# Second dispatch of a macaron layer: rounded products in place of plain ones, and the picks' weights on another engine

## The chip, the cores and the metric

The kernel runs on one core of one Trainium2 chip. The metric is the device time of one execution in microseconds (us). The five engines of the core work side by side and meet only at semaphores: TensorE (PE in the profile, with its weight loads as PEld), VectorE (DVE), ScalarE (ACT), GpSimd (POOL) and SyncE (SP, which issues transfers).

## The reference, cut to what matters

Three sublayers work on 8192 tokens of width 128: a mixture of experts, a linear attention, and the same mixture again. The change lies in the second mixture.

```python
x = x + 0.5 * ffn(layernorm(x))
x = x + attention(layernorm(x))
x = x + 0.5 * ffn(layernorm(x))

def ffn(x):                                # 8 routed experts of width 256, two picks a token
    shared = (silu(x @ shared_gate.T) * (x @ shared_up.T)) @ shared_down.T
    logits = x @ router_w.T + routing_bias
    scores, idx = top_k(sigmoid(logits), 2)
    scores = scores / scores.sum(-1)       # the weights of the picks
    w = scatter(scores at idx)
    combined = einsum((silu(x @ gate_w) * (x @ up_w)), down_w, w)
    return shared + combined
```

## The kernel before

The tokens are 16 tiles of 512 rows (TILES, TT), each of four sub-blocks of 128 (SUB). The program of each engine is written out by hand, in order; an engine does nothing ahead of its turn. There are five stages: the first dispatch (normalise, route, send each row to its two experts, shared expert), the first slot stage (72 slots of 256 rows through the routed experts), the middle, the second slot stage, and the last adds. The middle lies from about 355 to 575 us and runs the attention and the second dispatch (f = 1) together, in `TURNS`. In turn i the attention works on tile i, its projections on tile i+1, its transposes on tile i+2; the second dispatch transposes and routes tile i-1 (LAG_T) and runs the shared expert of tile i-2 (LAG_G).

Per turn, TensorE's order is: key_value(i), transpose of attention tile i+2, project(i+1, first half), ranks(i-2), gate_up(i-2, half 0), times_wo(i), transpose of dispatch tile i-1, project(i+1, second half), attend(i), router(i-1), query(i+1), gate_up(i-2, half 1), down_shared(i-3). The two halves of gate_up share one pair of banks here, so each waits for VectorE's multiply of the half before it.

VectorE's order is: mask_heads(i), add_bias(i) (the output bias), value(i+1, 0), add_late, the last steps of route for tile i-2 (from step 17 on), multiply half 0, value(i+1, 1), in some turns statistics of a late tile and three steps of the slot table, add_attention(i), norm_stats and variance for tile i, the first steps of route for tile i-1, shift_rows for tile i, in turns 4 and 8 a normaliser of four attention tiles (norm_late), multiply half 1, route up to the reciprocal (step 16), add_shared(i-3). Route is 25 small dependent steps (ROUTE_STEPS): 0 and 1 add the bias and the two column groups of the logits, 2 to 12 find the two best experts, 13 to 16 prepare the scores, 17 to 20 work out the places to which rows are sent, and 21 to 24 make the weights of the picks: product of ScalarE's Silu of the score and a reciprocal, sum of the two, reciprocal of that, and the product that is written into the rows to send.

POOL's order is, per tile: a copy of the row numbers, a wait for the whole route of that tile, four indirect transfers (first_rows) that send the rows, and then deviation: the power that makes 1/sqrt of the variance of the tile two further on, for which shift_rows waits.

ScalarE's order begins each turn with send_normalised(i-1), which needs shift_rows of the turn before, then high (the copy of the transposed attention tile), the Silu of the keys, the Silu of the scores (route_silu), the Silu of the gate, and so on.

In f = 1 the dispatch's products are plain f32 ones (the set PLAIN): `high` copies the transposed tile from tr_bank into a part of `pad`, and gate_up and router read it there as f32, the weights from `shared_raw` and `router_raw`. In f = 0 the same functions take another way: `high` copies it rounded (F32R) into xT_hi, VectorE's `low` writes the rest (the tile less xT_hi) into xT_lo, and each product is made of rounded parts: `three` is hi*hi, hi*lo and lo*hi of weights and data; the router takes two, against 16 columns that hold its weights' high and low parts. TensorE frees tr_bank for the next transpose when xT_hi is done (plain) or xT_lo is done (rounded).

Of the kernel before, what the change touches and what calls it, by code (L numbers as in the profile page):

```python
# [13 lines left out]
P = 128  # L14
# [21 lines left out]
XT_RING = 4  # L36
# [35 lines left out]
PLAIN = {(kind, 1, t) for kind in (ATTN, FFN) for t in range(TILES)}  # L72
SPLIT_BEFORE = {item: sum(other not in PLAIN for other in TRANSPOSED[:m]) for m, item in enumerate(TRANSPOSED)}
ROUTE_STEPS = 25
LOGITS_READ, MASK_STEP, SAFE_STEP, RECIP_STEP, RANKS_READ = 2, 13, 16, 17, 19
NORM_STEPS, POWER_STEPS = 10, 2
# [20 lines left out]
WARM_UP = 18  # L97
SECOND_PADDING_FROM = 22
# [16 lines left out]
def macaron(nc, x_in, w_experts, router_wT, routing_bias, w_attn, bq, bv, bo, out):  # L115
# [20 lines left out]
    with ExitStack() as ctx:  # L136
# [24 lines left out]
        shared_raw = sb("shared_raw", [P, 2 * INNER])  # L161
# [37 lines left out]
        neg_half = sb("neg_half", [P, WIDEST])  # L199
        attn_rstd = sb("attn_rstd", [P, tiles * SUB])  # L200
        attn_shift = sb("attn_shift", [P, tiles * SUB])
        xn = two("xn", [P, SUB, P])
        xT_hi = ring(XT_RING, "xT_hi", [P, TT], F32R)
        xT_lo = ring(XT_RING, "xT_lo", [P, TT], F32R)

# [101 lines left out]
        logits_psum, route_step, score_silu_done = sem("logits_psum"), sem("route_step"), sem("score_silu_done")  # L307
        ranks_psum, filled_reset = sem("ranks_psum"), sem("filled_reset")
# [51 lines left out]
        def xT_of(item):  # L360
            kind, f, t = item
            return xT_hi[t % XT_RING], xT_lo[t % XT_RING]

        def plain_xT(item):

            k = SUB * ((0 if item[0] == ATTN else 2) + item[2] % 2)
            return pad.rearrange("p e j d -> p (e j) d")[:, k:k + SUB, INPUT:RESULT]
# [117 lines left out]
        def _(sp):  # L485
# [11 lines left out]
            sp.dma_start(shared_raw[:], w_experts[0, :, 0:2 * INNER]).then_inc(attn_loaded, 16)  # L497
# [118 lines left out]
        def _(pool):  # L616
# [15 lines left out]
            pool.memset(neg_half[:], -0.5).then_inc(memsets, 1)  # L632
            pool.memset(before[:], 1.0).then_inc(memsets, 1)
            pool.memset(all_ones[:], 1.0).then_inc(memsets, 1)
            pool.wait_ge(memsets, 5)
# [7 lines left out]
            pool.wait_ge(memsets, 6)  # L643
# [23 lines left out]
            def ffn_tile(f, t):  # L667
                b = BATCH_OF[f][t]
                i = t - BATCHES[f][b][0]
                row_numbers(f, t)  # L670
                pool.wait_ge(route_step, (batch_no(f, b) + 1) * ROUTE_STEPS)
                pool.wait_ge(row_numbered, f * tiles + t + 1)
                pool.wait_ge(send_xn_done, f * tiles + t + 1)
                for j in range(SUB):
                    k = i * SUB + j
                    pool.indirect_dma_start(  # L676
                        first_rows, bass.IndirectOffsetOnAxis(ap=send_to[b % SEND_TO_RING][:, k:k + 1], axis=0),
                        send[ring_of(f, t)][:, j, :], None).then_inc(sent[ring_of(f, t)], 16)
                if f == 1 and t + LAG_G < tiles:
                    deviation(NORM_OF[(FFN, 1, t + LAG_G)][0])  # L680

# [47 lines left out]
        def _(act):  # L729
# [4 lines left out]
            def high(item):  # L734
                kind, f, t = item
                act.wait_ge(xT_psum, TR[item] + 1)
                if kind == ATTN:
                    wait_count(act, proj_psum, 3 * (t - 1))
                elif item in PLAIN:
                    act.wait_ge(gu_psum, 2 * (f * tiles + t - 2) + 2)  # L740
                elif f * tiles + t >= XT_RING:
                    act.wait_ge(gu_psum, 2 * (f * tiles + t - XT_RING) + 2)
# [36 lines left out]
            def route_silu(f, b):  # L779
                n = len(BATCHES[f][b]) * SUB  # L780
                act.wait_ge(route_step, batch_no(f, b) * ROUTE_STEPS + SAFE_STEP)
                act.activation(score_silu[:, :, 0:n], score_safe[:, :, 0:n], ACT.Silu).then_inc(score_silu_done, 1)
# [205 lines left out]
        def _(pe):  # L988
# [34 lines left out]
            def router(f, t):  # L1023
# [31 lines left out]
            def gate_up(n, c, par):  # L1055
# [32 lines left out]
            def gate_up_tile(f, t):  # L1088
                for c in range(HALVES):
                    gate_up(f * tiles + t, c, t % XT_RING)  # L1090
# [105 lines left out]
            def slot_stage(f):  # L1196
# [15 lines left out]
                if f == 0:  # L1212
                    pe.wait_ge(attn_loaded, 80)
# [75 lines left out]
            def middle():  # L1289
                first_turns()  # L1290
                for i in range(LAG_G, TURNS.stop):
# [9 lines left out]
                    if g:  # L1301
                        gate_up(tiles + i - LAG_G, 0, (i - LAG_G) % XT_RING)
# [12 lines left out]
                    if g:  # L1315
                        gate_up(tiles + i - LAG_G, 1, (i - LAG_G) % XT_RING)
# [12 lines left out]
        def _(dve):  # L1329
# [105 lines left out]
            def route(f, b, first, last):  # L1435
# [27 lines left out]
                plain = (FFN, f, ts[0]) in PLAIN  # L1463
                for step in range(first, last):
                    if plain and step == 0:
                        dve.wait_ge(logits_psum, batch_no(f, b) + 1)
                        dve.tensor_tensor(grid(z), logits[:, :, 0:ROUTED], by_expert(bias_b[:]), ALU.add
                                          ).then_inc(route_step, LOGITS_READ)
                    if plain and step < LOGITS_READ:
                        continue  # L1470
# [29 lines left out]
                    if step == 16:  # L1500
                        op = dve.reciprocal(picks(score_recip), picks(score_safe))
# [25 lines left out]
                    if step == 24:  # L1527
# [3 lines left out]
                            op0=ALU.mult, op1=ALU.mult)  # L1531
                    op.then_inc(route_step, 1)
# [250 lines left out]
            def dispatch():  # L1783
# [27 lines left out]
                for b in range(WRITTEN_OUT, len(BATCHES[f])):  # L1811
# [31 lines left out]
                    for t in ts:  # L1843
                        if t == tiles - 3:
                            dve.wait_ge(attn_loaded, 80)
# [147 lines left out]
            def first_turns():  # L1993
# [16 lines left out]
                variance(NORM_OF[(FFN, 1, 1)][0])  # L2010
                value(2, 1)
# [10 lines left out]
            def middle():  # L2022
                first_turns()
                for i in range(LAG_G, TURNS.stop):
# [7 lines left out]
                    if g:  # L2032
# [71 lines left out]
```

## Time and profile before

| | us |
|---|---|
| median of 3 runs | 793.89 (792.95 to 795.49) |
| the profiled execution, its own time | 791.14 |
| its span, first to last instruction | 789.4 |
| PE busy in the span | 694.9 (88%) |
| PEld busy | 629.6 (80%) |
| DVE busy | 551.2 (70%) |
| ACT busy | 462.1 (59%) |
| POOL busy | 453.7 (57%) |

Busy shares over the whole span mix five stages. The page's second part cuts the span into 40 slices of 19.7 us: slices 18 to 28 are the middle. There PE stands at 8 or 9 tenths and more, DVE at 8, ACT at 5 to 7 and POOL at 2 to 5. A start in the timelines is in us from the start of the span. A plain f32 product shows as two matmul records for each one written, a rounded one as one.

### The profile page before, as it was taken

Reading aid. Unit: us, or ns where it says so; the run is one execution under the profiler, and the core shown is the slowest. Engines: PE = TensorE matmul, PEld = TensorE weight load, DVE = VectorE, ACT = ScalarE, POOL = GpSimd, SP = SyncE. Lnnn points to the kernel's source line nnn. Section 1 sums busy time; section 2 is a strip of 40 time slices with the busy share of each in tenths; the row PEclk is TensorE's granted clock in tenths of the full one; section 3 lists DMA queues with packets and bytes.
Section 4 is the critical chain, followed back from the end, with each engine's and each line's share of the span. In section 5 each row is a group of like instructions: output and inputs, shape, how many; then the busy total and the mean of one; then the engine's idle time right before and its main releaser. Section 6 shows DMA issues by size and latency. Waiting matters only on the chain. (4 is left out here: it accounts for less than half of the span.)

```text
span 789.4 us, 18023 instructions
## 1 busy us (share of the span) xinstructions
PE 694.9 (88%) x5165; PEld 629.6 (80%) x5165; DVE 551.2 (70%) x1762; ACT 462.1 (59%) x849; POOL 453.7 (57%) x499
## 2 busy tenths in 40 slices
PE   4578859979999899999898999999789999899990
PEld 4466748869999899987676777777589999889990
DVE  6778887874555555688888888888865555555672
ACT  2325535237667657786775757755447677657760
POOL 5253666637777757765234353453527777667772
PEclk8579988989999999999999999999989999999995
DMA  9211164126788577651110000000427788476677
GB/s 277 84 44 42 55 165 118 43 83 190 206 246 220 167 190 196 176 168 48 51 50 30 22 28 18 26 28 19 110 71 220 215 233 241 143 195 170 186 238 232
DMA packets 88099, 103.52 MB, mean 131 GB/s; under 512 B 12228, under 2 KB 70468, under 8 KB 88004
## 3 DMA queue, kind: packets, MB, share of 16 engines
q1 hardware_dynamic: 72388, 65.23, 31.3%
q0 software_dynamic: 15616, 37.14, 13.1%
q8 instruction: 46, 0.75, 0.4%
q14 instruction: 49, 0.40, 0.2%
HBM read 51.83 MB, written 50.49 MB: 130 GB/s over the span
## 5 line engine op out<-in xcount | busy, mean ns | idle before, releaser
L676 POOL DMA_INDIRECT first_rows<-send,send_to x128 | 125.7, 982 | 170.6 <-DVE send L1528 135.9
L1862 DVE TENSOR_TENSOR h<-silu_g,u_bank 128x512 f32<-128x512 f32 x144 | 99.0, 688 | 142.8 <-ACT silu_g L870 138.4
L688 POOL DMA_INDIRECT second_rows<-row_ring x144 | 139.0, 965 | 67.5 <-issue 42.4
L688 POOL DMA_INDIRECT y_rows<-row_ring x144 | 141.2, 981 | 58.0 <-issue 35.7
L845 ACT ACTIVATE slot_gu<-w_gu 128x1024 fp32r x132 | 139.8, 1059 | 41.9 <-issue 41.8
L1190 PE MATMUL y_bank<-w_dn,h 128*128 x1152 | 151.7, 274 | 0.3 <-DVE h L1862 0.3
L1190 PEld LDWEIGHTS y_bank<-w_dn,h 128*128 128x128 f32 x1152 | 140.4, 191 | 0.5 <-issue 0.5
L991 PE MATMUL g_bank<-xT_hi,slot_gu 128*128 128x256 f32 x264 | 85.9, 325 | 12.7 <-DVE xT_lo L1853 12.7
L870 ACT ACTIVATE silu_g<-g_bank 128x512 f32<-128x512 f32 x144 | 83.6, 581 | 15.5 <-PE g_bank L993 15.4
L1084 PEld LDWEIGHTS y_bank<-w_dn,h 128*128 128x128 f32 x512 | 65.2, 202 | 23.2 <-issue 22.5
L1084 PE MATMUL y_bank<-w_dn,h 128*128 128x128 f32 x512 | 66.5, 286 | 13.2 <-DVE x L1427 13.2
L766 ACT ACTIVATE silu_g<-g_bank 128x512 f32<-128x512 f32 x64 | 38.2, 596 | 67.9 <-PE u_bank L993 43.2
L991 PE MATMUL u_bank<-xT_hi,slot_gu 128*128 128x256 f32 x264 | 75.1, 284 | 0.0
L992 PE MATMUL u_bank<-xT_lo,slot_gu 128*128 128x256 f32 x264 | 75.1, 284 | 0.0
L992 PE MATMUL g_bank<-xT_lo,slot_gu 128*128 128x256 f32 x264 | 74.7, 283 | 0.0
L993 PE MATMUL g_bank<-xT_hi,slot_gu 128*128 128x256 f32 x264 | 74.6, 282 | 0.0
L993 PE MATMUL u_bank<-xT_hi,slot_gu 128*128 128x256 f32 x264 | 74.3, 282 | 0.0
L775 ACT ACTIVATE send<-x,shift,rstd 128x128 f32<-128x128 f32 x128 | 52.1, 481 | 30.2 <-DVE shift L1405 22.6
L991 PEld LDWEIGHTS g_bank<-xT_hi,slot_gu 128*128 128x128 f32 x264 | 50.3, 191 | 14.6 <-DVE xT_lo L1853 14.6
L992 PEld LDWEIGHTS g_bank<-xT_lo,slot_gu 128*128 128x128 f32 x264 | 50.8, 192 | 0.0
L993 PEld LDWEIGHTS u_bank<-xT_hi,slot_gu 128*128 128x128 f32 x264 | 50.6, 192 | 0.0
L993 PEld LDWEIGHTS g_bank<-xT_hi,slot_gu 128*128 128x128 f32 x264 | 50.3, 190 | 0.0
(258 smaller groups left out, 1531.0 us busy)
## 6 DMA issues: line engine op xcount, KB each, us to landing
row_ring<-second_rows SPq DMA_DIRECT2D x66, 258.0 KB
row_ring<-first_rows SPq DMA_DIRECT2D x66, 132.0 KB
w_raw<-w_experts SPq DMA_DIRECT2D x21, 256.0 KB, 2.8
second_rows<-pad SPq DMA_DIRECT2D x16, 258.0 KB
x<-x_in SPq DMA_DIRECT2D x16, 256.0 KB, 7.0
xT_hi<-y_rows SPq DMA_DIRECT2D x16, 256.0 KB, 2.9
xT_lo<-y_rows SPq DMA_DIRECT2D x16, 256.0 KB, 2.9
out<-x SPq DMA_DIRECT2D x16, 256.0 KB
```

Source lines behind the costliest of these rows:

```text
L676: pool.indirect_dma_start(first_rows, bass.IndirectOffsetOnAxis(ap=send_to[b % SEND_TO_RING][:, k:k + 1], axis=0), send[ring_of(f, t)][:, ...
L688: pool.indirect_dma_start(to, bass.IndirectOffsetOnAxis(ap=rows[k][:, j, at:at + 1].bitcast(I32), axis=0), rows[k][:, j, columns], None).t ...
L766: act.activation(silu_g[c][:], g_bank[gate_bank(n, c)][:], ACT.Silu).then_inc(silu_done, 1)
L775: last = act.activation(send[ring_of(f, t)][:, j, INPUT:RESULT], x_sub(t, j), ACT.Identity, bias=bias, scale=scale)
L845: act.activation(slot_gu[n % 2][:].rearrange("p a n -> p (a n)"), w_gu[:, bass.ds(e, 1)].rearrange("p e a n -> p (e a n)").bitcast(F32), A ...
L870: act.activation(silu_g[n % 2][:], g_bank[n % 2][:], ACT.Silu).then_inc(slot_silu_done, 1)
L991: pe.matmul(bank_ap, w_parts[0], x_parts[0], start=True, stop=False)
L992: pe.matmul(bank_ap, w_parts[0], x_parts[1], start=False, stop=False)
L993: return pe.matmul(bank_ap, w_parts[1], x_parts[0], start=False, stop=True)
L1084: last = pe.matmul(shared_bank[:, s], h[t % 2][c][:, s], w_dn[:, 0, c, :], start=(c == 0), stop=(c == HALVES - 1))
L1190: last = pe.matmul(y_bank[par][:, j * P:(j + 1) * P], h[par][0][:, c * ROWS + j * P:c * ROWS + (j + 1) * P], w_dn[:, bass.ds(e[j % len(e)] ...
L1862: dve.tensor_tensor(h[par][0][:], silu_g[par][:], u_bank[par][:], ALU.mult).then_inc(slot_h_done, 1)
```

## The change

In the second dispatch the products of the shared expert and of the router become rounded ones, as in the first: PLAIN keeps only the attention's tiles. For that xT_hi and xT_lo are used as a ring of two, VectorE gets `low` for each tile (after multiply half 0, and once in first_turns), and route gets its step 0 and 1 apart instead of one add. Route on VectorE ends for f = 1 at step 20 and steps 21 to 24 go to POOL: `pick_weights`, five instructions, each of which waits for the one before it, placed in ffn_tile after the copy of the row numbers and before the wait for route. The reciprocal of the sum is there a power with the exponent -1, and the factor 0.5 is a multiplication of the sum by 2. ScalarE's route_silu and VectorE's step 16 wait for the weights of the tile before. The load of shared_raw falls away, with its wait. One constant (minus_one) is set at the start.

```diff
-XT_RING = 4
+XT_RING = (4, 2)
-PLAIN = {(kind, 1, t) for kind in (ATTN, FFN) for t in range(TILES)}
+PLAIN = {(ATTN, 1, t) for t in range(TILES)}
+PLACES_STEP = 20
+WEIGHT_STEPS = 5
...
-            sp.dma_start(shared_raw[:], w_experts[0, :, 0:2 * INNER]).then_inc(attn_loaded, 16)
...
+            pool.memset(minus_one[:], -1.0).then_inc(memsets, 1)
...
             def ffn_tile(f, t):
                 b = BATCH_OF[f][t]
                 i = t - BATCHES[f][b][0]
                 row_numbers(f, t)
+                if f == 1:
+                    pick_weights(t)
+                    pool.wait_ge(weights_step, WEIGHT_STEPS * (t + 1))
                 pool.wait_ge(route_step, (batch_no(f, b) + 1) * ROUTE_STEPS)
...
+            def pick_weights(t):
+                n = SUB
+                picks = [a[:, :, 0:n] for a in (score_silu, score_recip, prob)]
+                pool.wait_ge(score_silu_done, batch_no(1, t) + 1)
+                pool.wait_ge(route_step, batch_no(1, t) * ROUTE_STEPS + RECIP_STEP + 1)
+                pool.tensor_tensor(picks[2], picks[0], picks[1], ALU.mult).then_inc(weights_step, 1)
+                pool.wait_ge(weights_step, WEIGHT_STEPS * t + 1)
+                pool.tensor_tensor(total[:, 0:n], prob[:, 0, 0:n], prob[:, 1, 0:n], ALU.add).then_inc(weights_step, 1)
+                pool.wait_ge(weights_step, WEIGHT_STEPS * t + 2)
+                pool.tensor_scalar(total[:, 0:n], total[:, 0:n], 2.0, None, ALU.mult).then_inc(weights_step, 1)
+                pool.wait_ge(weights_step, WEIGHT_STEPS * t + 3)
+                pool.tensor_tensor(inv_total[:, 0:n], total[:, 0:n], minus_one[:], ALU.pow).then_inc(weights_step, 1)
+                pool.wait_ge(weights_step, WEIGHT_STEPS * t + 4)
+                wait_count(pool, sent[ring_of(1, t)], sent_count(1, t - SEND_RING))
+                pool.tensor_tensor(send[ring_of(1, t)][:, :, WEIGHT:WEIGHT + PICKS].rearrange("p s w -> p w s"), picks[2],
+                                   inv_total[:, 0:n].unsqueeze(1).to_broadcast([P, PICKS, n]), ALU.mult).then_inc(weights_step, 1)
...
             def route_silu(f, b):
                 n = len(BATCHES[f][b]) * SUB
                 act.wait_ge(route_step, batch_no(f, b) * ROUTE_STEPS + SAFE_STEP)
+                if f == 1:
+                    wait_count(act, weights_step, WEIGHT_STEPS * b)
...
-                    if (FFN, f, t) in PLAIN:
-                        last = pe.matmul(logits[:, 0:ROUTED], plain_xT((FFN, f, t))[:, j, :], router_raw[:], start=True, stop=True)
-                        continue
-                    pe.matmul(logits, xT_hi[t % XT_RING][:, s], router_parts[:], start=True, stop=False)
-                    last = pe.matmul(logits, xT_lo[t % XT_RING][:, s], router_parts[:], start=False, stop=True)
+                    hi, lo = xT_of((FFN, f, t))
+                    pe.matmul(logits, hi[:, s], router_parts[:], start=True, stop=False)
+                    last = pe.matmul(logits, lo[:, s], router_parts[:], start=False, stop=True)
...
-                if (FFN, 1, n - tiles) in PLAIN:
-                    xs = plain_xT((FFN, 1, n - tiles))
-                    pe.matmul(by_sub(g_bank[k][:]), shared_raw[:, c * P:(c + 1) * P], xs, start=True, stop=True)
-                    pe.matmul(by_sub(u_bank[k][:]), shared_raw[:, INNER + c * P:INNER + (c + 1) * P], xs, start=True, stop=True
-                              ).then_inc(gu_psum, 1)
-                    return
                 w = w_gu[:, 0]
-                xs = (xT_hi[par][:], xT_lo[par][:])
+                hi, lo = xT_of((FFN, n // tiles, n % tiles))
+                xs = (hi[:], lo[:])
...
                     if step == 16:
+                        if f == 1:
+                            wait_count(dve, weights_step, WEIGHT_STEPS * ts[0])
                         op = dve.reciprocal(picks(score_recip), picks(score_safe))
...
+                    if f == 1 and step == PLACES_STEP:
+                        op.then_inc(route_step, ROUTE_STEPS - PLACES_STEP)
+                        break
                     op.then_inc(route_step, 1)
...
                 variance(NORM_OF[(FFN, 1, 1)][0])
+                low((FFN, 1, 0))
                 value(2, 1)
...
                         if i - LAG_G == tiles - 1:
                             table_piece(1, "last tile")
+                    if tr:
+                        low((FFN, 1, i - LAG_T))
                     if 0 < i + 1 < tiles:
                         value(i + 1, 1)
```

## Rows read from the trace of the kernel before

**Rows 1.** Windows, one a turn: us, each engine's busy time, PE clock, DMA share, GB/s

```profile
402.84:414.87 12.03, 12.03 (x77) 9.34 (x77) 10.74 (x41) 8.61 (x19) 4.73 (x6) 1.00 0.20 64
414.87:429.98 15.11, 12.56 (x78) 9.36 (x77) 12.81 (x53) 8.37 (x19) 5.15 (x6) 1.00 0.07 23
...
516.89:528.92 12.03, 12.03 (x77) 9.34 (x77) 10.23 (x42) 7.25 (x15) 5.16 (x7) 1.00 0.07 24
```

**Rows 2.** Timeline of PE in one turn: start us, us, engine line op

```profile
455.17 1.02 PE L1063 MATMUL g_bank<-pad,shared_raw 128*128 128x512 f32 x2
...
456.88 1.95 PE L1084 MATMUL y_bank<-w_dn,h 128*128 128x128 f32 x16
...
461.01 1.10 PE L1063 MATMUL g_bank<-pad,shared_raw 128*128 128x512 f32 x2
...
462.81 0.61 PE L1254 MATMUL y_bank<-attn_raw,kv_sb 128*128 128x128 f32 x4
...
465.44 0.96 PE L1034 MATMUL route_bank<-router_raw,pad 128*128 128x8 f32 x8
466.26 1.10 PE L1237 MATMUL u_bank<-pad,attn_raw 128*128 128x512 f32 x2
```

**Rows 3.** Timeline of PE in the first dispatch, and the window over it

```profile
100.17 0.48 PE L991 MATMUL g_bank<-xT_hi,w_gu 128*128 128x512 f32 x1
...
103.06 1.95 PE L1084 MATMUL y_bank<-w_dn,h 128*128 128x128 f32 x16
...
105.19 0.26 PE L1036 MATMUL route_bank<-router_parts,xT_hi 128*128 128x16 f32 x1
...
106.09 0.66 PE L1013 MATMUL tr_bank<-ident,send 128*128 128x128 f32 x4
...
100.00:110.00 10.00, 9.54 (x65) 8.09 (x63) 9.13 (x27) 4.59 (x10) 7.70 (x9) 1.00 0.22 60
```

**Rows 4.** Timeline of DVE in the same turn as rows 2

```profile
453.54 0.68 DVE L1422 TENSOR_TENSOR h<-silu_g,u_bank 128x512 f32<-128x512 f32 x1
454.15 0.42 DVE L1914 TENSOR_TENSOR v_sb<-u_bank,bv_b 128x256 f32<-128x256 f32 x1
...
456.73 0.19 DVE L1467 TENSOR_TENSOR z<-route_bank,bias_b 128x32 f32<-128x32 f32 x1
456.96 0.19 DVE L1481 TENSOR_REDUCE score<-z 128x4 f32<-128x32 f32 x1
...
464.53 0.18 DVE L1519 TENSOR_REDUCE send_to<-pick_place 128x4 int32<-128x32 f32 x1
...
465.44 0.68 DVE L1422 TENSOR_TENSOR h<-silu_g,u_bank 128x512 f32<-128x512 f32 x1
```

**Rows 5.** Timeline of the loop through DVE, ACT and POOL, one turn

```profile
497.58 0.16 DVE L1405 SCALAR_TENSOR_TENSOR shift<-stats,rstd 128x4 f32<-128x4 f32 x1
...
500.07 0.20 ACT L782 ACTIVATE score_silu<-score_safe 128x8 f32<-128x8 f32 x1
...
502.91 1.06 POOL L676 DMA_INDIRECT first_rows<-send,send_to  x1 [5.22 <-DVE send L1528]
504.27 0.95 POOL L676 DMA_INDIRECT first_rows<-send,send_to  x1 [0.30 <-issue]
...
507.76 1.06 POOL L658 TENSOR_TENSOR rstd<-var,neg_half 128x4 f32<-128x4 f32 x1
```

**Rows 6.** POOL's small instructions: timeline, then lines' ns min/median/max

```profile
2.35 0.29 POOL L627 TENSOR_SCALAR_AFFINE_SELECT ident<-ident 128x128 f32<-128x128 f32 x1 [0.16 <-POOL ident L625]
...
L664 POOL COPY send<-number x32: 179/184/277, 13.8 to 564.5; 128x4 int32<-128x4 int32 x32
...
L658 POOL TENSOR_TENSOR rstd<-var,neg_half x17: 1046/1057/2959, 81.6 to 554.5; 128x4 f32<-128x4 f32 x15, 128x16 f32<-128x16 f32 x2
...
L694 POOL TENSOR_TENSOR w_gu<-w_raw,w_gu x8: 1266/1286/1308, 49.3 to 128.0; 128x512 fp32r<-128x512 f32 x8
```

**Rows 7.** Timeline of DVE at the end of the middle

```profile
560.78 0.19 DVE L1467 TENSOR_TENSOR z<-route_bank,bias_b 128x32 f32<-128x32 f32 x1 [0.60 <-PE route_bank L1034]
```

More of the change, by code:

```diff
@@ L97 @@
 WARM_UP = 18
+WEIGHT_STEPS = 5
+ATTN_LOADS = 4
 SECOND_PADDING_FROM = 22
@@ L160, in macaron @@
         slot_gu = two("slot_gu", [P, 2, 2 * INNER], F32R)
-        shared_raw = sb("shared_raw", [P, 2 * INNER])
         attn_raw = sb("attn_raw", [P, 4 * P])
@@ L199, in macaron @@
         neg_half = sb("neg_half", [P, WIDEST])
+        minus_one = sb("minus_one", [P, SUB])
         attn_rstd = sb("attn_rstd", [P, tiles * SUB])
@@ L202, in macaron @@
         xn = two("xn", [P, SUB, P])
-        xT_hi = ring(XT_RING, "xT_hi", [P, TT], F32R)
-        xT_lo = ring(XT_RING, "xT_lo", [P, TT], F32R)
+        xT_hi = ring(XT_RING[0], "xT_hi", [P, TT], F32R)
+        xT_lo = ring(XT_RING[0], "xT_lo", [P, TT], F32R)
         send_ring = sb("send", [P, SEND_RING, SUB, RESULT])
@@ L307, in macaron @@
         logits_psum, route_step, score_silu_done = sem("logits_psum"), sem("route_step"), sem("score_silu_done")
+        weights_step = sem("weights_step")
         ranks_psum, filled_reset = sem("ranks_psum"), sem("filled_reset")
@@ L361, in xT_of @@
             kind, f, t = item
-            return xT_hi[t % XT_RING], xT_lo[t % XT_RING]
+            return xT_hi[t % XT_RING[f]], xT_lo[t % XT_RING[f]]
         def plain_xT(item):
-            k = SUB * ((0 if item[0] == ATTN else 2) + item[2] % 2)
+            k = SUB * (item[2] % 2)
             return pad.rearrange("p e j d -> p (e j) d")[:, k:k + SUB, INPUT:RESULT]
@@ L632, in _ @@
             pool.memset(neg_half[:], -0.5).then_inc(memsets, 1)
+            pool.memset(minus_one[:], -1.0).then_inc(memsets, 1)
             pool.memset(before[:], 1.0).then_inc(memsets, 1)
             pool.memset(all_ones[:], 1.0).then_inc(memsets, 1)
-            pool.wait_ge(memsets, 5)
+            pool.wait_ge(memsets, 6)
             pool.affine_select(out=before[:], in_=before[:], compare_op=ALU.is_ge, fill=0.0, base=-1,
@@ L642, in _ @@
                                pattern=[[-HEAD, HEADS], [0, HEAD]], channel_multiplier=1).then_inc(memsets, 1)
-            pool.wait_ge(memsets, 6)
+            pool.wait_ge(memsets, 7)
             pool.affine_select(out=heads, in_=heads, compare_op=ALU.is_ge, fill=0.0, base=HEAD - 1,
@@ L738, in high @@
                     wait_count(act, proj_psum, 3 * (t - 1))
[L739 to L742, printed above, removed]
+                elif f * tiles + t >= XT_RING[f]:
+                    act.wait_ge(gu_psum, 2 * (f * tiles + t - XT_RING[f]) + 2)
                 if item in PLAIN:
@@ L1053, in ranks, with gate_up @@
                 last.then_inc(ranks_psum, 1)
-            def gate_up(n, c, par):
+            def gate_up(n, c):
                 k = gate_bank(n, c)
@@ L1089, in gate_up_tile @@
                 for c in range(HALVES):
-                    gate_up(f * tiles + t, c, t % XT_RING)
+                    gate_up(f * tiles + t, c)
             def dispatch():
@@ L1212, in slot_stage @@
                 if f == 0:
-                    pe.wait_ge(attn_loaded, 80)
+                    pe.wait_ge(attn_loaded, 64)
                     project(0, 0)
@@ L1301, in middle @@
                     if g:
-                        gate_up(tiles + i - LAG_G, 0, (i - LAG_G) % XT_RING)
+                        gate_up(tiles + i - LAG_G, 0)
                     if attn:
@@ L1315, in middle @@
                     if g:
-                        gate_up(tiles + i - LAG_G, 1, (i - LAG_G) % XT_RING)
+                        gate_up(tiles + i - LAG_G, 1)
                     if 0 <= i - LAG_G - 1 < tiles - 1:
@@ L1461, in chosen @@
                     return mask[len(ts)][:, 0:n, w * ROUTED:(w + 1) * ROUTED]
-                plain = (FFN, f, ts[0]) in PLAIN
                 for step in range(first, last):
[L1465 to L1470, printed above, removed]
                     if step > 0:
@@ L1844, in dispatch @@
                         if t == tiles - 3:
-                            dve.wait_ge(attn_loaded, 80)
+                            dve.wait_ge(attn_loaded, 64)
                             dve.tensor_scalar(bq_scaled[:], bq_col[:], SCALE, None, ALU.mult).then_inc(bq_ready, 1)
```

## The prediction

> **What bounds the kernel now.** I read the page's 40 slices first, to find the stage that the edit touches, and then only that stage: the windows cut at the start of each query product, so that one window is one turn; after that the timelines of PE, DVE and POOL inside one turn. The change touches the middle alone (the second dispatch runs there, between 355 and 575 us), so whatever bounds the slot stages stays as it is.
>
> [...] The reader is to see that two turns 114 us apart have the same 12.03 to the hundredth: a stage that waits for data wanders, one that is bound by an engine doesn't. DVE is busy for 10.2 to 10.7 us of it, and between its 41 or 42 instructions lie gaps of some 0.04 where one depends on the other [rows 1, 4], so DVE is close behind. Turn 4 is another kind: 15.11 us, PE busy for 12.56 and idle for the rest, because VectorE's normaliser of four tiles stands ahead of a multiply that PE needs; turn 8 is the same. Nine turns are ordinary ones (the first and the eighth of them stand in rows 1), two are long; three come ahead of them and two behind, where the pipeline fills and drains.
>
> A third thing is nearly as long as the turn: a loop through three engines. Shift_rows at 497.58 lets ScalarE normalise the next tile; behind that in ScalarE's order stands the Silu of the scores, which ends at 500.27; then come VectorE's places and weights, POOL's first transfer at 502.91, three more, and the power at 507.76, which ends at 508.82 and lets the next shift_rows go [rows 5]. That is 11.27 us with a hop of 0.03. It is not what ends last now, but it has under 0.8 us to spare.
>
> **The change part by part.**
>
> Gate and up on PE. Now the two halves of a tile take 456.88 - 455.17 = 1.71 and 462.81 - 461.01 = 1.80, together 3.51 us [rows 2]. Rounded, the same two halves took 103.06 - 100.17 = 2.89 us in the first dispatch, with the clock at 1.00 there too [rows 3]. So a turn of PE loses 0.62 us.
>
> Router on PE. Now 466.26 - 465.44 = 0.82 [rows 2]; rounded, 106.09 - 105.19 = 0.90 [rows 3]. It gains 0.08. PE's turn becomes 12.03 - 0.62 + 0.08 = 11.49 us, 0.54 less. Over nine turns that is 4.9 us, if nothing else is longer than 11.49.
>
> VectorE. It gains `low`, a 128x512 instruction out of PSUM; the multiply of that size holds the engine for 454.15 - 453.54 = 0.61. It gains one more step of route, 456.96 - 456.73 = 0.23. It loses steps 21 to 24: the multiply behind them starts at 465.44, the last step that stays starts at 464.53 and takes 0.18, and an instruction that doesn't depend on it may follow before its end, so between 0.73 and 0.91 goes, and I take 0.8 [rows 4]. The net is +0.04 a turn, between -0.07 and +0.11. I take nothing for it in the ordinary turns, where PE covers it, and 0.1 in all for the two long ones. If that cover is gone, eleven turns cost 0.4 us.
>
> The wait that is new on PE. Router needs `low`, and `low` stands behind multiply half 0. Now router and multiply start together, both at 465.44 [rows 2, 4]. After the change router can't start before multiply and low are through: 0.61, 0.68 for low as for the multiply, and a hop of 0.05, so 1.34 us after the multiply's start. Behind it on PE's queue wait query, gate_up half 1 and down_shared; for gate_up half 1 waits multiply half 1, which VectorE reaches only behind 13 steps of route, so VectorE isn't held up. PE pays this once, when the order first settles (turns 1 to 3, where DVE is behind), and keeps the distance from then on: PE's own way from gate_up half 0 to router (1.80 - 0.31, then times_wo, transpose, project and attend, 462.81 to 465.44 in rows 2) is 4.1 us, and behind the half's 1.49 Silu, multiply, high and low, each of some 0.6 to 0.7, two of them side by side on two engines, fit into it. Cost +1.3 us, once; between 0 (VectorE is early, so that low is done first) and 2.5 (it is paid again behind each long turn). I take 1.3.
>
> The weights on POOL. Five instructions that wait for one another and for the Silu of the scores, ahead of the four transfers and the power. The trace shows no such form of POOL with eight columns. The nearest rows: a copy of four columns 0.18 (median), a power of four columns 1.06, a dependent gap of 0.16, a two-input subtraction of 512 columns 1.29, which is 2.5 ns a column, so that eight columns are next to nothing and the fixed part counts [rows 6]. Below: four at 0.18 and a power, no gaps: 1.8 us. Above: four at 0.29 (the 128-column select) with a gap of 0.16 each, the power and its gap: 3.0 us. I take four at 0.21, gaps of 0.1 to 0.16, the power 1.06: 2.4 us. The loop is then 500.27 - 497.58 = 2.69, the weights 2.4, the issue gap of 0.30 that lies before a transfer, and from the first one's start to the next shift (the power's end and the hop) 508.85 - 502.91 = 5.94: 11.33 us [rows 5]. It stays under PE's 11.49 by a hair; the cover is gone from 2.56 us of weights on. VectorE's own route doesn't wait for the weights any more, and places (step 20) are done before them.
>
> [...]
>
> The end of the middle. Tile 15's routing is the chain: VectorE waits for the router's logits before 560.78 [rows 7], and all that follows, up to the slot table, is VectorE's. On it come low and its hop, 0.75, and one step, 0.23; off it go half a gate_up ahead of the transpose, 0.31, and steps 21 to 24, 0.8: -0.1 us.
>
> The rest. The transfer of shared_raw lies among the first loads, away from the chain: nothing. ScalarE's high writes the same 512 columns: nothing. The memset lies before POOL's first wait: nothing.
>
> The sum: -4.9 + 1.3 + 0.1 - 0.1 = -3.6 us. The profiled execution took 791.14 us, its span 789.4 and 1.7 around it; it would become 787.5. It is itself 2.75 under the median of the three runs, 793.89. Against that median, which is what the change will be compared with, I forecast 790.3 us.
>
> **The rivals.**
>
> POOL's loop becomes the bound, mildly. With weights of 2.6 to 3.1 us the loop is 11.5 to 12.0, and nine turns gain between 4.9 and 0.3; with the 1.3 the total runs from -3.6 to +1.0, say 793 us. For it: the loop is already 11.27 and the new instructions all depend on one another [rows 5]. Against: with a price in the middle of the bounds the loop stays under PE's turn, and VectorE's places and weights no longer stand between the Silu and the first transfer in one queue.
>
> POOL's loop becomes the bound, hard: slower. If the weights take 3.5 us, the loop is 12.43, longer than the turn of before: nine turns at +0.4, and 1.3 and -0.1: +4.8, 798.7 us. It decides from weights of about 3.2 us on. [...] Against it: every short instruction of POOL in the trace lies under 0.3 us and the power varies by 1% at four columns [rows 6].
>
> The router's wait costs nothing and VectorE follows PE at once: -6 us and somewhat more, 787.5 us. For it: VectorE sheds its weights just before the multiply, so the multiply comes earlier by 0.8. Against: in rows 2 and 4 the two start together, so low is late by more than that.
>
> The change doesn't shorten PE: the rounded products keep to 2.89 us in the first dispatch where PE isn't pressed; in the middle their weight loads (three per product instead of two) could stand in the way, and a turn stays near 12.0. Then only the costs are left, +1, 795 us. Against: there PE ran them back to back with the loads beside them [rows 3].
>
> **How the numbers follow.** Forecast 0.52 at 790.3 us, its own spread 788.5 to 792.5 by the bounds of VectorE's net and of the router's wait. Mild loop 0.22 at 793; hard loop 0.10 at 798.7; more gained 0.11 at 787.5; no shorter PE 0.05 at 795. A measurement of this kernel tells about 0.3%, 2.4 us, from no change, so faster means under 791.5: four fifths of the forecast's chance, all of the larger gain and a little of the mild loop: 0.55. Slower, over 796.3: the hard loop and a little beside: 0.11. Between: 0.34. The range from 786.5 to 796.5 leaves out most of the hard loop and the far end of the larger gain, together under 2 in 10.
>
> **What would show it.** Right: windows cut at query are 11.4 to 11.6 us in the nine turns, PE busy throughout; gate_up's two halves 2.9 us together; router starting right behind xT_lo, some 1.3 us after multiply half 0; POOL's five instructions 2.2 to 2.6 us from the Silu's end to the last. Wrong: DVE idle before shift_rows for POOL's power in every turn, and turns of 11.8 us or more (the loop); PE idle before router in every turn, with DVE busy throughout (VectorE's order is the bound); long turns that grow by more than 0.2.

## The result, and the profile after

The changed kernel takes 810.75 us (median of 4 runs, 808.08 to 811.89), beside 793.42 (791.95 to 795.49, 4 runs) for the kernel before: a ratio of 1.021, interval 1.0165 to 1.0256. The forecast was 790.3, up to 796.5. The profiled execution has a span of 809.1 us, 19.7 more than before.

Nearly all of it lies in the middle. The windows cut at the query products, as in [rows 1] (columns: us, busy time of PE, PEld, DVE, ACT and POOL with their instructions, PE clock, DMA share, GB/s); the last line is the tail, from the last query to the second slot stage's first `low`:

```profile
437.90:450.91 13.01, 12.04 (x82) 10.15 (x81) 10.72 (x40) 8.56 (x19) 7.06 (x11) 1.00 0.06 21
504.99:517.39 12.40, 12.03 (x82) 10.15 (x81) 10.33 (x41) 8.56 (x19) 7.07 (x11) 1.00 0.07 23
517.39:529.79 12.40, 12.04 (x82) 10.15 (x81) 10.04 (x40) 8.56 (x19) 7.06 (x11) 1.00 0.07 23
554.60:594.94 40.34, 29.60 (x173) 25.12 (x172) 29.71 (x121) 13.60 (x27) 24.25 (x36) 0.87 0.27 71
```

Turns of 12.40 us in a row, and of 13.0 where a late tile is added; before, both kinds took 12.03 to 12.21. The same to the hundredth from turn to turn, and yet PE isn't busy throughout: something else than PE sets it. The waits over the whole middle name it (columns: us in total, times, longest):

```profile
POOL prob L694 <- DVE place L1518: 71.6, 16, 8.8
...
DVE shift L1422 <- POOL rstd L662: 21.3, 14, 2.2
```

The second of them in the kernel before:

```profile
DVE shift L1405 <- POOL rstd L658: 4.3, 7, 1.0
```

So before, VectorE's shift_rows waited 4.3 us in all for POOL's power; now it waits 21.3. The loop of [rows 5], in one turn after:

```profile
511.01 0.16 DVE L1422 SCALAR_TENSOR_TENSOR shift<-stats,rstd 128x4 f32<-128x4 f32 x1 [1.28 <-POOL rstd L662]
...
513.50 0.20 ACT L806 ACTIVATE score_silu<-score_safe 128x8 f32<-128x8 f32 x1
...
514.23 0.22 DVE L1518 TENSOR_TENSOR place<-route_bank,filled 128x64 f32<-128x64 f32 x1
...
514.60 0.20 POOL L694 TENSOR_TENSOR prob<-score_silu,score_recip 128x8 f32<-128x8 f32 x1 [3.46 <-DVE place L1518]
514.88 0.20 POOL L696 TENSOR_TENSOR total<-prob 128x4 f32<-128x4 f32 x1
515.17 0.23 POOL L698 TENSOR_SCALAR total<-total 128x4 f32<-128x4 f32 x1
515.48 1.04 POOL L700 TENSOR_TENSOR inv_total<-total,minus_one 128x4 f32<-128x4 f32 x1
516.59 0.21 POOL L703 TENSOR_TENSOR send<-prob,inv_total 128x8 f32<-128x8 f32 x1
517.40 1.11 POOL L683 DMA_INDIRECT first_rows<-send,send_to  x1 [0.60 <-POOL send L703]
...
522.31 1.06 POOL L662 TENSOR_TENSOR rstd<-var,neg_half 128x4 f32<-128x4 f32 x1
...
523.40 0.16 DVE L1422 SCALAR_TENSOR_TENSOR shift<-stats,rstd 128x4 f32<-128x4 f32 x1 [1.60 <-POOL rstd L662]
```

From shift to the Silu's end 513.70 - 511.01 = 2.69, as before. Then 0.90 in which nothing of the loop runs on POOL; the weights, 516.80 - 514.60 = 2.20; a gap of 0.60; and 523.40 - 517.40 = 6.00 to the next shift. Together 12.39: this is the turn. The 0.90 is the surprise, and the row names its cause: the first weight waits for VectorE's place add. `pick_weights` waits for `RECIP_STEP + 1` = 18 steps of route, so for steps 0 to 17. The reciprocal, which it needs, is step 16; it is done at a count of 17, and 17 is what the constant `RECIP_STEP` holds. Step 17 is the place add, and this stands on VectorE behind add_shared, mask_heads, add_bias, value and, in the turns with a late tile, an add_late.

### The profile page after: what moved, and what is told of

It reads as the page before. It is cut to its first block, busy times and chain, and to the rows that moved or that the text cites. A ratio compares the mean times of both kernels' runs of the same rounds, so it can differ in the third digit from the quotient of the medians.

```text
span 809.1 us, 18241 instructions
## 1 busy us (share of the span) xinstructions
PE 704.3 (87%) x5229; PEld 652.7 (81%) x5229; DVE 553.4 (68%) x1730; ACT 461.8 (57%) x849; POOL 485.5 (60%) x580
## 4 chain that ended last, share of the span: by engine, by line
PE 42%; POOL 18%; DVE 13%; issue 9%; DMA 3%; ACT 3%; SPq 1%; POOLq 0%; DVEq 0%; ACTq 0%
PE y_bank L1207 11%; POOL first_rows L683 6%; POOL second_rows L712 6%; PE g_bank L1015 4%; PE g_bank L1017 3%; PE g_bank L1016 3%; PE u_bank L1015 3%; PE u_bank L1016 3%; PE u_bank L1017 3%; PE y_bank L1101 3%; DMA row_ring<-second_rows 2%; POOL rstd L662 2%; POOL inv_total L700 2%; DVE h L1439 2%; PE route_bank L1161 1%
## 5 line engine op out<-in xcount | busy, mean ns | idle before, releaser
L1016 PEld LDWEIGHTS u_bank<-xT_lo,slot_gu 128*128 128x128 f32 x264 | 50.5, 191 | 0.0
```

Of the source, the lines that this page charges most:

```text
L1016: pe.matmul(bank_ap, w_parts[0], x_parts[1], start=False, stop=False)
```

## The experiments

All compared with the kernel before on the same chip. For each profiled execution I cut the middle by the starts of the query products on PE: the first four turns; the nine ordinary turns of the prediction; the two long ones; and the tail. Medians and ratios come from the timed runs; the stretches (us) from one profile each. The kernel before had a median of 793.42, 792.1, 794.15 and 792.34 us in the four sessions: beside the changed kernel, e1 to e4, e5 to e8, and e9 and e10.

| kernel | first four | nine ordinary | two long | tail | middle | median | ratio (interval) |
|---|---|---|---|---|---|---|---|
| before | 38.13 | 108.04 | 29.64 | 34.08 | 209.89 | 793.42 | |
| changed | 41.53 | 114.63 | 31.92 | 40.34 | 228.42 | 810.75 | 1.021 (1.0165 to 1.0256) |
| e1_wait16 | 40.63 | 107.99 | 29.89 | 37.83 | 216.34 | 797.67 | 1.006 (1.0033 to 1.0087) |
| e2_products | 43.61 | 108.18 | 30.81 | 36.48 | 219.08 | 800.45 | 1.0102 (1.0063 to 1.0141) |
| e3_weights | 40.50 | 111.06 | 34.21 | 38.76 | 224.53 | 809.4 | 1.0202 (1.0157 to 1.0246) |
| e4_weights16 | 37.44 | 108.60 | 30.16 | 34.28 | 210.48 | 794.67 | 1.0028 (1.0004 to 1.0052) |
| e5_after_early | 41.90 | 102.63 | 29.44 | 34.38 | 208.35 | 788.89 | 0.9944 (0.9918 to 0.9969) |
| e6_before_early | 38.14 | 107.85 | 27.85 | 33.20 | 207.04 | 790.09 | 0.9954 (0.9928 to 0.9979) |
| e7_wait16_early | 41.88 | 102.62 | 29.36 | 34.27 | 208.13 | 789.82 | 0.9941 (0.9919 to 0.9962) |
| e8_plain_router | 38.08 | 102.00 | 29.29 | 34.31 | 203.68 | 786.22 | 0.9917 (0.9885 to 0.9948) |
| e10_router_alone | 39.74 | 106.87 | 29.74 | 38.89 | 215.24 | 795.4 | 1.0033 (1.0004 to 1.0063) |

### The wait, and each half of the change

**e1_wait16**, the changed kernel with one number less:

```diff
-                pool.wait_ge(route_step, batch_no(1, t) * ROUTE_STEPS + RECIP_STEP + 1)
+                pool.wait_ge(route_step, batch_no(1, t) * ROUTE_STEPS + RECIP_STEP)
```

> The changed kernel, but POOL's first weight instruction waits for step 16 of route (the reciprocal) and not for step 17 (the places), which VectorE makes only behind value and the late add. Theory A (the loop through shift_rows, ScalarE, VectorE's places, POOL's weights, transfers and power sets the turn, 12.40 us, and 13.0 where a late tile is added): the first weight instruction starts 0.8 us earlier in ordinary turns and 1.4 in those with a late add, turns of 11.5 to 11.7 us, 794 to 798 us in all. Theory B (low ahead of router, with VectorE as the bound, is what costs): turns stay at 12.4 and more, 808 to 812 us.

12 us of the middle come back (228.42 to 216.34). POOL now waits for ScalarE's Silu, and starts 0.08 behind its end (518.47):

```profile
518.27 0.20 ACT L806 ACTIVATE score_silu<-score_safe 128x8 f32<-128x8 f32 x1
...
518.55 0.26 POOL L694 TENSOR_TENSOR prob<-score_silu,score_recip 128x8 f32<-128x8 f32 x1 [2.66 <-ACT score_silu L806]
...
521.48 1.17 POOL L683 DMA_INDIRECT first_rows<-send,send_to  x1 [0.61 <-POOL send L703]
```

The ordinary turns are 11.69 to 11.84, those with a late add 12.0: theory A holds. But 797.67 is still 7 above the forecast, so the wait isn't all.

**e2_products** leaves the weights on VectorE: the call of `pick_weights` and all waits for it go, and route runs to step 24 again.

```diff
-                if f == 1:
-                    pick_weights(t)
-                    pool.wait_ge(weights_step, WEIGHT_STEPS * (t + 1))
...
-                    if f == 1 and step == PLACES_STEP:
-                        op.then_inc(route_step, ROUTE_STEPS - PLACES_STEP)
-                        break
```

> Rounded products and low as in the change, but the weights stay on VectorE (steps 21 to 24), POOL as before. Theory A: POOL's loop is that of before, VectorE has 0.8 us more a turn than in the change, turns of 11.4 to 12.3 us, 792 to 797 us in all. Theory B (low ahead of router costs): 803 us or more, TensorE idle ahead of router in each turn.

It lands between the two, so neither theory had the total: the rounded products alone cost 9.2 us in the middle, 5.5 of it in the first four turns. In the sum the nine ordinary turns gain nothing, but they aren't alike: the first takes 14.03, the next three 12.11 to 12.13, the last five 11.38 to 11.82. The loop isn't what costs here, since shift_rows waits only 0.3 us in all for the power. What theory B named does: TensorE waits ahead of the router for `low`, 13 times and 14.9 us in all over the middle. One of the first waits, and the sum from 400 to 560 us:

```profile
393.67 0.38 PE L1053 MATMUL route_bank<-router_parts,xT_hi 128*128 128x16 f32 x1 [3.40 <-DVE xT_lo L1428]
...
PE route_bank L1053 <- DVE xT_lo L1428: 8.6, 10, 1.8
```

**e3_weights** does the other half: products plain as before, weights on POOL with the change's wait. **e4_weights16** is the same with the wait for step 16. Both are the kernel before with only the weights' part of the change. Seen from the changed kernel, the products' part is taken back, of which this line is the core:

```diff
-PLAIN = {(ATTN, 1, t) for t in range(TILES)}
+PLAIN = {(kind, 1, t) for kind in (ATTN, FFN) for t in range(TILES)}
```

> Plain products as before, the weights on POOL with the change's own waits. Theory A: the loop is as long as in the change, 12.4 us in ordinary turns and 13.0 with a late add, though VectorE has 0.8 us less work a turn: 801 to 807 us. Theory B: 792 to 794 us, since TensorE's turn of 12.03 and its order are those of before.

> Plain products as before, the weights on POOL, which wait for step 16 only. Theory A: the loop is 11.5 to 11.6 us and lies under TensorE's turn of 12.03: 792 to 795 us. Theory C (any work on POOL ahead of the transfers lengthens the turn by as much): 11.27 and the difference of POOL's and VectorE's weights, turns above 12.03, 797 us or more.

By the ratios, the weights cost 16 us with the one wait and 2 with the other, in a kernel that has none of the rounded products. The long turns alone grow by 4.6 us in e3_weights, the tail by 4.7. So one number in one wait carries most of the loss. e3_weights went over its expected 801 to 807, and not in the ordinary turns, which I had counted. In its later ordinary turns the loop takes 12.41 us, as theory A says:

```profile
509.52 0.16 DVE L1431 SCALAR_TENSOR_TENSOR shift<-stats,rstd 128x4 f32<-128x4 f32 x1 [0.50 <-POOL rstd L662]
...
521.93 0.16 DVE L1431 SCALAR_TENSOR_TENSOR shift<-stats,rstd 128x4 f32<-128x4 f32 x1 [1.17 <-POOL rstd L662]
```

But TensorE keeps its 12.03 there and is busy throughout. VectorE falls behind it by 0.4 us a turn, and the loss shows in the stretches that wait for VectorE: the turns with a late add (12.6 to 13.0), the long turns and the tail.

### The loop

If the loop is the cause, it can be cut elsewhere: the power that closes it doesn't need the transfers in front of it, only VectorE's variance. **e5_after_early** (on the changed kernel, step 17 still waited for), **e6_before_early** (on the kernel before) and **e7_wait16_early** (on e1_wait16) all have this edit:

```diff
                         send[ring_of(f, t)][:, j, :], None).then_inc(sent[ring_of(f, t)], 16)
-                if f == 1 and t + LAG_G < tiles:
-                    deviation(NORM_OF[(FFN, 1, t + LAG_G)][0])
+                    if f == 1 and t + LAG_G < tiles and j == 1:
+                        deviation(NORM_OF[(FFN, 1, t + LAG_G)][0])
```

> The changed kernel, with POOL's power for the tile after next issued behind the second of the four transfers instead of behind the fourth; the weights still wait for step 17. Theory L (the changed kernel's 12.40 us turn is the loop shift, Silu, weights, transfers, power, shift): two transfers and their gaps, 2.5 us, leave the loop, which becomes 9.9; the turn falls to what PE or VectorE want, 11.5 to 11.9, VectorE's shift waits for the power in hardly any turn, and the total falls from 809 to 796-801. Theory W (late weights cost through something else: the transfers land late, or the clock is low for a reason of its own): the turns stay at 12.2 or more and the total at 805 or more.

> The kernel before, with the same power issued behind the second transfer. Theory L: the loop is 11.27 us there and PE's turn 12.03, so ordinary turns stay at 12.03 to the hundredth; only the places where VectorE's shift waits for the power (4.3 us over the middle, 0.8 of it next to the end) can give something: 790-793, within 0.3%. Rival: if the loop did bind somewhere that I read as PE's, the total falls by 3 us or more.

> The changed kernel with the weights waiting for step 16 (as in the first run) and the power behind the second transfer. Theory L: with 11.70 and 12.01 us the loop set the turns of the first run still, by the issue gap of 0.60 and PE's 11.6; without it the ordinary turns are 11.5 to 11.6, the turns with a late add 11.6 to 11.8, the end of the middle 1.3 shorter: 3 to 4 us less than the first run, 793-795. Rival R (what is left of the loss is the router's wait for low and the clock that falls behind it): turns fall by 0.1 at most in all but a few, and the total stays at 796-799.

In e5_after_early the loss is gone and more, though the weights start as late as in the changed kernel (POOL still waits 49.8 us in all for the place add). So late weights cost nothing by themselves; they cost through the loop. With the loop cut, the number in the wait no longer matters: the middles of e5_after_early and e7_wait16_early differ by 0.2 us. With e7_wait16_early the turns are 11.38 to 11.40, PE busy for all of them:

```profile
447.69:459.07 11.38, 11.38 (x81) 10.08 (x81) 10.69 (x40) 8.46 (x19) 7.62 (x12) 1.00 0.08 26
...
495.88:507.27 11.39, 11.39 (x82) 10.08 (x81) 10.40 (x41) 8.57 (x19) 7.23 (x11) 1.00 0.08 25
```

In e1_wait16 the loop still set the turns: 2.69 + 0.08 + 2.32 + 0.61 + 6.0 = 11.7. Both kernels ended below what I expected: the ordinary turns came to 11.4 and not 11.5 or more, and the tail of e7_wait16_early is 3.6 us shorter than that of e1_wait16, where I expected 1.3. And e6_before_early, where I expected 0.3% at most, is 0.46% faster, the middle 2.85 us shorter: the ordinary turns stay at 12.03 as expected, but the long turns lose 1.8 (0.44 of it the turn of 15.11) and the tail 0.9. The loop did bind the kernel before, in turns I had read as VectorE's alone.

This makes e6_before_early the kernel to set e7_wait16_early against, since both have the early power. Against it the corrected change gains nothing: 789.82 beside 790.09 us in the same session, and a middle of 208.13 beside 207.04. The nine ordinary turns gain 5.2 us, and the first four (3.7), the long ones (1.5) and the tail (1.1) take them back. That e5_after_early and e7_wait16_early lie below the kernel before is the power's doing.

### The router's wait

What is left in e7_wait16_early is the first four turns, 3.75 us longer than before. PE's timeline there:

```profile
381.69 0.28 PE L1058 MATMUL route_bank<-router_parts,xT_hi 128*128 128x16 f32 x1 [0.55 <-DVE xT_lo L1433]
...
394.18 0.29 PE L1058 MATMUL route_bank<-router_parts,xT_hi 128*128 128x16 f32 x1 [2.59 <-DVE xT_lo L1433]
...
395.61 0.36 PE L1059 MATMUL route_bank<-router_parts,xT_lo 128*128 128x16 f32 x1
395.82 2.06 PE L1254 MATMUL u_bank<-pad,attn_raw 128*128 128x512 f32 x2
...
408.11 0.28 PE L1058 MATMUL route_bank<-router_parts,xT_hi 128*128 128x16 f32 x1 [0.83 <-DVE xT_lo L1433]
```

Three waits for `low`, 4.0 us in all. Behind the long one PE runs slow: the query's two products take 2.06 us instead of the 1.10 of [rows 2], with a granted clock of 0.50 from 395.82 to 397.90, and the turn from 395.82 has a mean of 0.80.

**e8_plain_router** is e7_wait16_early with the router on a plain copy of the tile (a second copy by ScalarE, ahead of the rounded one), and gate_up alone rounded; VectorE's route has one step less again, as with plain products:

```diff
+                    if f == 1:
+                        act.activation(plain_xT(item), by_sub(tr_bank[:]), ACT.Copy).then_inc(plain_done, 1)
                     act.activation(xT_of(item)[0][:], tr_bank[:], ACT.Copy).then_inc(xT_hi_done, 1)
...
+                if f == 1:
+                    pe.wait_ge(plain_done, t + 1)
+                else:
+                    wait_xT((FFN, f, t))
...
+                    if f == 1:
+                        last = pe.matmul(logits[:, 0:ROUTED], plain_xT((FFN, f, t))[:, j, :], router_raw[:], start=True, stop=True)
+                        continue
...
+                if n >= tiles and c == 0:
+                    wait_xT((FFN, 1, n - tiles))
```

> The kernel of the run before this, with only gate and up in three rounded products: ScalarE copies the transposed tile twice (plain for the router, then rounded), the router takes the plain copy and waits for no low; VectorE's route loses its extra step. Theory R (the router's wait for low costs the first turns and the end of the middle): PE's idle time before the router goes, the first turns are near those of before, the end of the middle is 2 us shorter, and the total is 787-792, under the run before this by 2 us or more. Theory L alone: within 1.5 us of the run before this, or above it because ScalarE has 0.6 us more in every turn.

3.6 us under e7_wait16_early, and the first four turns are back at 38.08, those of before. The windows of its third, fourth and a later turn:

```profile
382.35:393.11 10.76, 8.74 (x59) 7.17 (x58) 9.43 (x43) 9.52 (x22) 2.59 (x7) 1.00 0.08 27
393.11:405.70 12.59, 10.23 (x64) 8.22 (x64) 11.78 (x40) 8.83 (x20) 7.48 (x11) 1.00 0.24 60
...
444.09:455.46 11.37, 11.37 (x81) 10.08 (x81) 10.72 (x39) 8.94 (x20) 7.91 (x12) 1.00 0.08 26
```

The clock stays at 1.00 in these turns. In the same four turns the window of e7_wait16_early that holds the slow stretch reads:

```profile
395.82:409.02 13.20, 12.37 (x64) 10.00 (x65) 9.51 (x37) 8.27 (x19) 6.25 (x10) 0.80 0.10 30
```

So the theory of the router's wait holds for the first turns. It doesn't for the end of the middle: the tail is 34.31 beside 34.27 us, where the theory wanted 2 us less. At 786.22 us, a ratio of 0.9917, this kernel is the only one with rounded products that is clearly below e6_before_early, by 3.9 us between the medians of one session.

**e10_router_alone** has e8's router, but the power behind the fourth transfer again: do the two losses add up?

> The kernel with the weights waiting for step 16 and the router on a plain copy, the power again behind the fourth transfer. It asks whether the two losses add up. Theory: they do; the router's wait is worth 3.5 to 4.5 us in the first four turns, as between the two runs with the early power, and the loop of 11.70 us (12.0 beside a late add) stays the bound of the turns that follow, so it ends 3 to 5 us under the first run: 793-795. Rival (the loop hides what the router gives, because a turn that is bound by the loop gains nothing from a PE that waits less): 796-798.

They don't. Against e1_wait16 the second and third turn together give 2.5 us back, and the fourth takes 1.6 of them again (14.24 after 12.67); the middle is 1.1 us shorter, not 4. In the later turns the shift waits for the power as before:

```profile
503.26 0.16 DVE L1432 SCALAR_TENSOR_TENSOR shift<-stats,rstd 128x4 f32<-128x4 f32 x1 [0.72 <-POOL rstd L662]
```

The median, 795.4, lies just below the rival's 796 to 798; by the stretches the rival is nearer.

**e9_copy_last** asks what the 0.60 before the first transfer are. It is e7_wait16_early with `row_numbers(f, t)` moved from before `pick_weights(t)` to behind it; one run, 789.3 us.

> The kernel with step 16 and the early power, its copy of the row numbers moved from before the five weights to behind them, so that an independent POOL instruction stands between the last weight and the first transfer. It asks what the 0.60 us before that transfer are, where the traces had 0.30 behind VectorE's write. Theory a (a transfer waits 0.60 behind whatever POOL wrote last): 0.60 again, now behind the copy, and the first transfer starts 0.2 to 0.3 later after the last weight's end than the 0.60 of before. Theory b (0.60 belongs to the last weight's write): the copy lies inside the 0.60, and the idle time shown behind it is 0.3 to 0.4. The total is 789-791 either way, since the loop has over 1 us to spare there.

```profile
503.59 0.21 POOL L704 TENSOR_TENSOR send<-prob,inv_total 128x8 f32<-128x8 f32 x1
503.74 0.19 POOL L668 COPY send<-number 128x4 int32<-128x4 int32 x1
504.80 1.11 POOL L684 DMA_INDIRECT first_rows<-send,send_to  x1 [0.88 <-POOL send L668]
```

0.88 behind the copy: 1.00 from the last weight's end to the transfer, 0.40 more. Theory b wanted 0.3 to 0.4 there and falls. Theory a wanted 0.60 again: a gap does stand behind what POOL wrote last, but it isn't a fixed one. What it is made of stays open.

## Why the prediction was wrong

**What failed: the start of the weights.** The prediction's loop runs from the Silu's end straight into the weights, and says that the places "are done before them". So the sum has nothing between the Silu and the first weight, and the runs showed 0.90 us there. I read the threshold as the reciprocal's step, 16. It is the place add, 17, and in VectorE's order four other instructions, or five, stand between the two. With the 0.90 the prediction's own sum is 12.23 instead of 11.33; with every term as measured it is 2.69 + 0.90 + 2.20 + 0.60 + 6.00 = 12.39, and the condition "under PE's 11.49 by a hair" turns round. The trace of before shows the distance already: in the turn of [rows 5] the place add starts 0.53 us behind the Silu's end.

```profile
500.80 0.22 DVE L1506 TENSOR_TENSOR place<-route_bank,filled 128x64 f32<-128x64 f32 x1
```

From shift_rows to the place add it is 3.22 us there, and 3.22 in the turn after: up to the place add this part of the loop is VectorE's own order, not the way through ScalarE's Silu.

The prediction also takes a turn that repeats to the hundredth for the sign of an engine as the bound. The changed kernel's 12.40 repeats as exactly, with PE busy for 12.03 of it: a loop repeats too.

**The weights' length was right**: 2.20 to 2.32 us measured in the ordinary turns, 2.4 forecast from [rows 6]. The longest in any run is 3.02 (e8_plain_router, from 413.56), so no run shows the 3.5 us of the hard rival's sum. **The gap was mis-sized**: 0.60 instead of 0.30. I took the gap between two transfers [rows 5]; the first one follows a POOL write. This alone would have brought the loop to 11.6, over PE's turn; e1_wait16 shows 11.7.

**The price of the loop was sized for nine turns only.** The hard rival had a loop of 12.43 us, and put it at +4.8. A loop of 12.40 came, and the middle grew by 18.5: 3.4 in the first four turns, 6.6 in the nine ordinary ones, 2.3 in the long ones and 6.3 in the tail. Cutting the loop and nothing else (changed kernel to e5_after_early) takes 20.1 us off the middle, 12.0 of it in the nine turns, where the gain on PE was hidden as well, and 6.0 in the tail, in which the loop turns twice more. The turns with a late add were dearer, because the place add stands behind that add too. And [rows 1] with its turn of 15.11 was read as VectorE's normaliser alone; e6_before_early shows that the power held the two long turns by 1.8 us already.

**PE's gain was right.** Forecast 11.49 from 12.03; measured 11.38 to 11.40 once nothing else binds. Half 0 of gate_up takes 1.48 there instead of 1.80 (502.34 to 503.82 in e7_wait16_early), the router 0.89 instead of 0.82, as [rows 3] had them. Nine turns give 108.04 - 102.62 = 5.4 us, forecast 4.9. The rival that PE isn't shortened falls with it. But the forecast took these 4.9 us for the kernel's, and they didn't reach the total, as e6_before_early and e7_wait16_early show.

**The router's wait was mis-sized**: 1.3 us "once", up to 2.5; in the first four turns of e7_wait16_early it is paid three times, 4.0 us of waiting and 3.75 net. In those turns VectorE has late adds and a normaliser ahead of multiply and low, which the estimate from one ordinary turn left out. It had no term for the clock, which was granted at 0.50 to 0.54 behind the longest of them (394.18 to 400.00). That PE keeps its distance in the ordinary turns was right: no wait in those of 11.38 to 11.40. In the turn ahead of them, the long turns and the tail it waits again, five times and 3.5 us; e8_plain_router, which has none of these waits, is no shorter in the long turns and the tail, so nothing shows that they cost time there.

**VectorE's net and the end of the middle** were right only for the ordinary turns, where PE is busy throughout in e7_wait16_early. Beside e6_before_early, which has the early power too, the two long turns are 1.5 us longer (forecast 0.1 longer) and the tail 1.1 longer (forecast 0.1 shorter). PE idles 4.9 us in these long turns instead of 3.1. A likely reason is that they wait for VectorE, and a PE that arrives earlier only waits longer; no run tests it.

**POOL's price for the small steps** was near VectorE's: in the changed kernel's turn shown above the two-input steps take 0.20 to 0.21 us on POOL for 4 and 8 columns, beside 0.16 to 0.17 for their like on VectorE in the kernel before (501.83 to 502.61). The weights were not slower than forecast; they were later.

The lower clock is not settled (0.87 in the changed kernel's tail). In the stretches read it stands behind idle time of PE, and not only behind the router's wait: e8_plain_router has 0.89 in its first long turn, in which PE waits 1.88 us for VectorE's multiply and has a clock of 0.50 from 427 to 430. But idle time alone doesn't tell it: behind a wait of 1.91 us in the same run, before 400.08, the clock stays at 1.00. What it costs apart from the idling no run separates.

## What to carry to other kernels

Before a step is moved to another engine, read the number in its wait against the other engine's order, instruction by instruction: a count that is one too high waits for the next instruction there, and that may stand behind a microsecond of other work. Follow every loop that the moved step lengthens through all kinds of turns, the first ones and the tail too, not only the ordinary one. And if a loop has to be shortened, look first at what stands in front of its closing instruction for no reason of data: here, moving one power ahead of two transfers gave 20 us back in the changed kernel, and 3 in the kernel before. Such a cut has to be made in the kernel before as well, or its gain is put down to the change.

## What the runs showed of the hardware

A transfer that follows the last weight, a POOL write of its own data, begins 0.60 us behind it (changed kernel, e1_wait16), one that follows another transfer 0.30, and one behind the power, whose result it doesn't read, 0.20 (e7_wait16_early); behind the copy of the row numbers, which also writes into these rows, it was 0.88 (e9_copy_last).

After 2.59 us of idling in e7_wait16_early PE's next products took about twice their time: router products 0.21 apart instead of the 0.11 of a later turn (506.38 to 506.93), the query's pair 2.06 instead of 1.10. The granted clock was 0.54 over those router products (394.18 to 395.82) and 0.50 from there to 400.00.

That the engines "meet only at semaphores" isn't what the times show. In e1_wait16 a small POOL instruction that fell beside a VectorE add of two tensors in SBUF took 0.59 us instead of 0.23, and ended 0.08 to 0.09 behind that add, in all four turns where the two fell together (416.50, 444.67, 456.68, 468.69). One of them:

```profile
456.51 0.68 DVE L1792 TENSOR_TENSOR x<-xT_lo,x 128x512 f32<-128x512 f32 x1
...
456.68 0.59 POOL L698 TENSOR_SCALAR total<-total 128x4 f32<-128x4 f32 x1
```

It ended at 457.27, VectorE's add at 457.19. The 0.36 are in the loop, and are about the step from turns of 11.7 to 12.0 in that kernel. The earlier start of the weights is what brought the two side by side: in the changed kernel, where they start behind the add, the same instruction takes 0.23 in those turns. Only at 390.72, in an early turn, it lies there beside VectorE's add of the bias (390.69 to 391.37), and takes 0.75. Why it takes longer beside such an add no run shows.
